# Position table by half-array products, no bias by TensorE in the steady batches, second norm a batch later, last batch written out

## The reference

```
qkv = LN(x) @ W_qkv + b_qkv                      # 16 heads of 8
scores = q k^T / sqrt(8) + rel_bias[clip(i - j + 128, 0, 256)]
attn = softmax(scores) v ; y = attn @ W_out + b_out
x = x + LN(y)
h = silu(LN(x) @ w1^T * s1) * (LN(x) @ w2^T * s2)      # 128 -> 512
h = gelu(h @ h1^T * h1s) ; h = gelu(h @ h2^T * h2s)    # 512 -> 512, ternary weights
x = x + LN(h @ w3^T * w3s)                       # 512 -> 128
```

## Time and profile before

| | before |
|---|---|
| median of 3 runs | 291.06 us (290.31 to 291.15) |
| the profiled execution | 290.61 us, its span in the trace 288.8 us |
| mean granted clock of TensorE | 0.992 |
| busy: PE, DVE, ACT, POOL | 267.7, 212.5, 205.2, 102.5 us |

### The profile page before, as it was taken

How to read it: one execution, slowest core, us unless ns; L and a number is a source line. 1 busy time by engine, 2 the same in 40 slices (tenths; PEclk the granted TensorE clock), 3 DMA queues, 4 the chain that set the end, 5 groups by cost and what they waited for, 6 DMA issues and landing times.

```text
span 288.8 us, 5174 instructions
## 1 busy us (share of the span) xinstructions
PE 267.7 (93%) x1875; PEld 180.7 (63%) x1875; DVE 212.5 (74%) x442; ACT 205.2 (71%) x316; POOL 102.5 (35%) x107
## 2 busy tenths in 40 slices
PE   7899989899999999999999998999999999999980
PEld 7656646555555555556555554557888888888860
DVE  4576977889789789789788888857654853673675
ACT  2677777785876776785886886767459976896750
POOL 6716000101702603923974985117640202400111
PEclk9999999999999999999999999999999999999996
DMA  6979505322221262560221200000000000010012
GB/s 159 339 231 142 184 5 183 129 65 90 64 84 41 74 194 103 179 210 21 75 78 36 78 0 3 1 3 1 0 2 0 0 0 2 0 36 2 2 36 77
DMA packets 21356, 21.17 MB, mean 73 GB/s; under 512 B 3664, under 2 KB 18768, under 8 KB 21072
## 3 DMA queue, kind: packets, MB, share of 16 engines
q1 hardware_dynamic: 20464, 20.53, 24.4%
q10 hardware_dynamic: 864, 0.27, 0.4%
HBM read 14.90 MB, written 5.64 MB: 71 GB/s over the span
## 4 chain that ended last, share of the span: by engine, by line
PE 68%; DVE 16%; ACT 8%; issue 5%; DMA 1%; POOL 1%; ACTq 0%; POOLq 0%; DVEq 0%
PE place L1449 11%; PE place L1450 11%; PE place L1252 10%; PE pv L1304 7%; DVE mx L692 6%; PE place L1244 5%; ACT ring L1016 4%; PE place L1278 4%; DVE place L699 3%; PE place L1203 2%; PE misc L1315 2%; PE place L1289 2%; PE misc L1182 2%; PE pv L1450 2%; PE pv L1449 2%
## 5 line engine op out<-in xcount | busy, mean ns | idle before, releaser
L692 DVE TENSOR_REDUCE mx<-place 128x4 f32<-128x1024 f32 x64 | 78.3, 1223 | 16.2 <-PE place L1252 14.9
L517 POOL TENSOR_TENSOR rstd<-mv,mhalf 128x2 f32<-128x2 f32 (+1 forms) x26 | 20.9, 806 | 145.8 <-DVE mv L624 145.8
L1016 ACT ACTIVATE ring<-place 128x1024 f32<-128x1024 f32 x64 | 65.7, 1028 | 6.4 <-PE place L1289 3.1
L1252 PE MATMUL place<-room,identr 128*128 128x512 f32 x128 | 47.0, 448 | 0.0
L1023 ACT COPY place<-raw 128x1024 f32<-128x1024 f32 x37 | 37.8, 1024 | 11.7 <-DVE mx L692 11.7
L1449 PE MATMUL place<-room,w_hi 128*128 128x512 f32 (+1 forms) x116 | 44.7, 387 | 0.7 <-DVE room L825 0.7
L1450 PE MATMUL place<-room,w_hi 128*128 128x512 f32 (+1 forms) x116 | 44.1, 383 | 0.0
L1304 PE MATMUL pv<-ring,vx 128*9 128x256 f32 x512 | 33.6, 380 | 0.4 <-ACT ring L1016 0.4
L825 DVE TENSOR_TENSOR room<-ring,room 128x512 fp32r<-128x512 f32 x32 | 21.3, 690 | 17.1 <-ACT room L1104 17.1
L1244 PE MATMUL place<-room 33*128 33x256 f32 x256 | 28.4, 298 | 4.9 <-ACT ring L1016 4.8
L1278 PE MATMUL place<-room 33*128 33x256 f32 x256 | 31.7, 328 | 1.4 <-DVE place L699 1.1
(11 more groups left out here) (141 smaller groups left out, 434.4 us busy)
## 6 DMA issues: line engine op xcount, KB each, us to landing
raw<-ext SPq DMA_DIRECT2D x8, 384.0 KB, 6.8
room<-q_parts SPq DMA_DIRECT2D x48, 64.0 KB
room<-k_parts SPq DMA_DIRECT2D x48, 64.0 KB
w_lo<-h SPq DMA_DIRECT2D x2, 1024.0 KB, 5.6
q_parts<-w_hi SPq DMA_DIRECT2D x4, 256.0 KB, 3.0
k_parts<-w_hi SPq DMA_DIRECT2D x2, 512.0 KB, 3.4
xs<-x SPq DMA_DIRECT2D x3, 256.0 KB, 6.1
w_lo<-w SPq DMA_DIRECT2D x3, 256.0 KB, 2.8
```

The source lines that it names most:

```text
L517: nc.gpsimd.tensor_tensor(rstd[:, at:at + width], mv[:, at:at + width, 1], mhalf[:, 0:width], ALU.pow).then_inc(rstd_set, 1)
L692: nc.vector.tensor_reduce(mx[:, s // RPAIRS, :, :, s % RPAIRS].rearrange("p i k -> p k i"), max_tile(b * PAIRS + s)[:, :, :].rearrange("p ...
L1016: nc.scalar.activation(probs[:, s % PRING, :, :, :].rearrange("p k j n -> p (k j n)"), score_tile(b * PAIRS + s)[:, :, :].rearrange("p k n ...
L1252: last = mm(max_tile(b * PAIRS + s)[:, half, :], identr[:, :], windows(table_hi[:, 2 * s + half, :], 0, P, 2, S), start=False, stop=True, ...
```

## The change

1. **Max bias in halves** (`bias_product`). The table holds, for head 0 of a pair, 64 partitions x 448 columns in partitions 0 to 63, and for head 1 the same in 64 to 127 (`load_halves`). The identity `ident_wide` is 64 rows x [zeros, identity, zeros]. Four products of 64 rows and 512 columns take the place of two of 128 rows.
2. **No bias by PE** in batches 0 to 6: for s = 7 ACT copies it too (a sixth copy in each batch). In the last batch PE does s = 6.
3. **Table loads.** The half tables (16 loads, into the free end of `w_lo`) come first; the full `raw` (8 loads) is loaded after `store_parts(1)` and ahead of `row_dmas(1)`.
4. **z a batch later.** Two places for z; `norm_T`, `keep_zT` and `z_low` run for batch b-2.
5. **The last batch** is written out on PE, DVE and ACT; DVE copies the bias of steps 1, 2, 3, 4, 5 and 7; `BLANKS` go from (2, 2, 2, 6, 6) to (0, 0, 0, 2, 6), and three blank streams stand elsewhere (4 products in b = 0, 4 in b = 5, 2 in b = 6).

```diff
-BY_PE = (7,)
+BY_PE = ()
 BY_DVE = (2, 5)
-LAST_BY_DVE = (1, 2, 4, 5, 6)
+LAST_BY_PE = (6,)
+LAST_BY_DVE = (1, 2, 3, 4, 5, 7)
...
-        BLANKS = (2, 2, 2, 6, 6)
+        BLANKS = (0, 0, 0, 2, 6)
...
+        def load_halves(eng, s):
+            for half in range(2):
+                eng.dma_start(raw_halves[half * HP:(half + 1) * HP, s, :],
+                              bass.AP(tensor=ext.tensor, offset=(2 * s + half) * EXT,
+                                      ap=[[1, HP], [1, TWIN]])).then_inc(table_in[s], 16)
...
             store_parts(1)
+            for s in range(PAIRS):
+                load_table(sp, s)
             sp.wait_ge(parts_out[1], PARTS_OUT)
             row_dmas(1, 0, PAIRS, second_rows_in)
...
+            def bias_product(tile, table, s, block, half):
+
+                at = half * HP
+                return mm(tile[:, half, :], ident_wide[at:at + HP, HP - block * HP:3 * HP - block * HP],
+                          windows(table[at:at + HP, s, :], block * HP, P, 2, S), start=False, stop=True,
+                          skip_group_check=True)
+
             def max_bias(b, s):
                 if b == 0:
                     pe.wait_ge(table_hi_pool, s + 1)
-                for half in range(2):
-                    last = mm(max_tile(b * PAIRS + s)[:, half, :], identr[:, :],
-                              windows(table_hi[:, 2 * s + half, :], 0, P, 2, S),
-                              start=False, stop=True, skip_group_check=True)
+                for block in range(2):
+                    for half in range(2):
+                        last = bias_product(max_tile(b * PAIRS + s), table_hi, s, block, half)
                 last.then_inc(ms_ready, 1)
...
             def second_norm(b):
                 dve.wait_ge(rstd_set, b * 2 + NU + 2)
-                if b > 0:
-                    dve.wait_ge(zT_ready, b)
+                if b > 1:
+                    dve.wait_ge(zT_ready, b - 1)
                 for t in range(TPB):
-                    last = normalize(z[:, t, :], xs[:, b * TPB + t, :], t)
+                    last = normalize(z[b][:, t, :], xs[:, b * TPB + t, :], t)
...
+            first = (B - 1) * PAIRS
+            write_bias(first + 2)
+            weigh(B - 2, 0)
+            write_bias(first + 3)
+            write_bias(first + 4)
+            write_bias(first + 5)
+            weigh(B - 2, 1)
+            largest_low()
+            write_bias(first + 7)
+            attn_moments(B - 2)
+            any_low()
+            residual(B - 2)
+            z_low(B - 3)
+            second_norm(B - 2)
...
+            last_scores(6)
+            weighted(B - 1, 2)
+            last_scores(7)
+            project(B - 2)
+            pe.wait_ge(y_read, B - 1)
+            pe.wait_ge(w_low_top_set, 2)
+            mm(misc[0:1, 0:P], w_low_top[:, :], ident[:, :], start=True, stop=True).then_inc(w_low_row, 1)
+            pe.wait_ge(w_low_any_set, 1)
+            norm_T(B - 3)
+            weighted(B - 1, 3)
```

More of the change, by code:

```diff
@@ L55 @@
 SLOT_HEAD = [s + HALF * k for s in range(PAIRS) for k in range(2)]
[L58 removed]
+BY_PE = ()
 BY_DVE = (2, 5)
[L60 to L61 removed]
+LAST_BY_PE = (6,)
+LAST_BY_DVE = (1, 2, 3, 4, 5, 7)
+LOW_PAIRS = BY_PE + tuple(s for s in LAST_BY_PE if s not in BY_PE)
 def windows(ap, start, step, count, width):
@@ L239, in build @@
         rows_set = sem("rows_set")
+        table_in = [sem(f"table_in{s}") for s in range(PAIRS)]
         table_hi_pool = sem("table_hi_pool")
@@ L1038, in _ @@
             write_bias(0)
-            for b in range(B):
+            for b in range(B - 1):
                 for s in range(PAIRS):
                     ahead = b * PAIRS + s + 1
-                    if ahead < B * PAIRS and ahead % PAIRS in by_act(ahead // PAIRS):
+                    if ahead % PAIRS in by_act(ahead // PAIRS):
                         write_bias(ahead)
@@ L1279, in scores @@
                                   rows(k_rows, b, half, s)[:, j * P:(j + 1) * P], rows(q_rows, b, half, s),
[L1280 to L1281 removed]
+                                  start=(s in by_pe(b) and j == 0), stop=False, skip_group_check=True)
+                if s not in by_pe(b):
                     last.then_inc(st_ready, 1)
             def score_bias(b, s):
[L1285 to L1290 removed]
+                low = LOW_PAIRS.index(s)
+                pe.wait_ge(table_lo_set, low + 1)
+                for table, at in ((table_hi, s), (table_lo, low)):
+                    for block in range(2):
+                        for half in range(2):
+                            last = bias_product(score_tile(b * PAIRS + s), table, at, block, half)
                 last.then_inc(st_ready, 1)
@@ L1360, in _ @@
             v(2)
-            for b in range(B):
-                more = b + 1 < B
+            for b in range(B - 1):
                 for s in range(PAIRS):
-                    if more or s not in BY_PE:
-                        scores(b, s)
-                    if s == 6 and 1 <= b <= 4:
+                    scores(b, s)
+                    if s == 6 and b > 0:
                         pe.wait_ge(mrow_set, b * RANGES + 3)
@@ L1376, in _ @@
                             v(4)
-                    if more:
-                        max_scores(b + 1, s)
-                        max_bias(b + 1, s)
-                    if s in BY_PE and more:
+                        if b == 5:
+                            stream(misc, blank, blank, 4)
+                        if b + 2 == B:
+                            norm_T(b - 2)
+                    max_scores(b + 1, s)
+                    max_bias(b + 1, s)
+                    if s in BY_PE:
                         score_bias(b, s)
-                    if s + 1 in BY_PE and not more:
-                        scores(b, s + 1)
-                        score_bias(b, s + 1)
                     if s == 0:
@@ L1426, in _ @@
                             v(3)
-                    if s == 5 and more:
+                    if s == 5:
                         if b == 0:
```

199 lines of the change are left out of this document (125 added, 74 removed).

## The result

Slower: 299.2 us in the median of four runs (295.6 to 302.9) against 291.0 for the kernel before beside it, a ratio of 1.025 (95% interval 1.021 to 1.028). The prediction was 284.3, with 280.5 to 289.5 as its range. Ratios here rest on the undisturbed runs of both kernels, so they can differ a little from the ratio of the medians. The profiled execution took 299.58 us, its span 297.8.

The account below looks back on a forecast made before the run. PE, two thirds of the chain, with DVE close behind it, was taken to bound the kernel. Start 0, batches -1.3 - 1.1 - 3 x 1.5 - 2 x 0.3, last batch +0.5 + 0.3 gave -6.7 us: 284.3, range 280.5 to 289.5.

Parts of the forecast that it names:

- 19.5 or 19.6: Predicted batch length in us, with DVE busy over 90%; step 7's exponentials 19.5 us apart in batches 1 to 6.
- The copy by ACT: Step 7: ACT's sixth copy is hidden and L1289's 0.94 us leaves the chain, starting the exponential 0.93 us sooner.
- third rival: Max bias: half products do not overlap, so the kernel gets slower, +8 us to 299; chance 0.06.
- z a batch later: 0: Step 7: the later z takes PE's transposes and DVE's z_low off fresh data, which stood in DVE's pause; 0 us.
- The start: 0 to 33 us: PE gains about 0 and some 6 us of slack cover the table loads; 0, bounds -0.5 and +3.
- First scores after 35: Start: a stated sign that the prediction is wrong; it expected first scores at 33.3 us.
- the early queue ends some 3.9 us sooner: Start, DMA: half tables are 1.8 MB where full ones are 3.1, at 340 GB/s.
- fourth rival: Start: loads back and the maxima's row land 5 to 8 us late behind the tables; 290 to 293 us, chance 0.08.
- The blank streams taken out lay in waits: Last batch: the removed blank streams stood in PE's waits; no time was counted for them.
- the steps on step 7 and on z: Batches: L1289's 0.94 us leaves the chain in batches 0 to 4; moving z's transposes a batch later counts 0.
- "+0.5" and "+0.3": Last batch: first FFN product 0.5 us later, then DVE's residual and second_norm +0.3; bounds -1 and +2.
- the estimate of 190.5: Last batch: project starts at about 190.5 us, from six copies, eight exponentials and job order; first FFN product at about 194.4.

Follow-up runs that it names:

- e6: e5 with the last batch in its order of before the change and z of batch 5 transposed in batch 6's step 7; 283.28 us, ratio 0.974.
- e7: The kernel before, max bias in full rows, with ACT's sixth copy and four zero products at step 7 in batches 0 to 6; 287.8 us, ratio 0.989.
- e3: The kernel before with only BY_PE = (): ACT copies the bias of step 7 in every batch, no half products; 294.9 us, ratio 1.017.
- e10: e6 with z transposed in the batch after it, as before the change; 283.26 us.
- e4: The changed kernel with the half tables of two pairs in one load, 8 issues for 16; 294.1 us, ratio 1.010.
- e1: The changed kernel with the eight full table loads issued behind the first maxima's row; 294.8 us, ratio 1.015.
- e2: The kernel before plus six 384 KB table loads, read by nobody, behind store_parts(1); 291.14 us, ratio 1.001.
- e5: e1b with e4's merged loads and batch 1's maxima row sent ahead of W_out's loads and unit 3's stores; 288.9 us, ratio 0.990.
- e1b: e1 with four zero products at step 7 of batches 0 to 6 and more blank streams in the rebuilt last batch; 291.55 us, ratio 1.001.
- e8: e6 without the added zero products (two in batch 6 stay); four runs of 283.7 to 295.8 us, ratio 0.984 without the longest.
- e9: e5 with six zero products ahead of each of the last batch's weighted sums; 289.6 us, ratio 0.995.

## Why the prediction was wrong

**What held: the length of the batches, in part by luck.** "19.5 or 19.6" was 19.40 in every undisturbed batch 2 to 4. In e6, with the clock up throughout, batches 0 to 6 gained 1.5, 1.2, 1.7, 1.7, 1.7, -0.1 and 0.4, together 8.1 us where the steps said 7.5. But the two terms behind this sum were both off. The copy by ACT, counted at some 0.93 us in each of batches 0 to 4 (4.7 in all), brought 0.4 to 1.0 in each, 2.8 in all (e7 and e3 alike). The rest of the change to the steady batches, for which that leaves 2.8 of the forecast's 7.5, brought 5.3 (e6 against e7). The errors cancel; no run shows why the halves bring more than their borders. That pairs of half products overlap did hold. PE's timeline after, in batch 3:

```profile
105.45 0.40 PE L1320 MATMUL place<-room 33*128 33x256 f32 x4
105.69 0.63 PE L1327 MATMUL place<-room 64*128 64x512 f32 x4
106.25 0.66 PE L1397 MATMUL misc<-ident,oT 128*128 128x128 f32 x4
...
107.18 0.40 PE L1320 MATMUL place<-room 33*128 33x256 f32 x4
107.42 0.63 PE L1327 MATMUL place<-room 64*128 64x512 f32 x4
107.98 0.40 PE L1386 MATMUL pv<-ring,vx 128*9 128x256 f32 x4
```

From L1320 to the weighted sum is 107.98 - 107.18 = 0.80 (0.81 predicted, 0.99 in the earlier trace rows), so pairs of half products overlap fully, and the third rival falls. Into a transpose it is 106.25 - 105.45 = 0.80 as well, not the 0.91 predicted: the extra 0.10 for a change of weights behind the max bias did not come, and the transposes gain 0.09 too. DVE is busy 91% of batch 3's window, as said (85% and 87% in e6's batches 2 and 6, though), and PE 18.2 us, not 17.5.

**z a batch later: 0.** e10 shows it, within 0.4 us. It does take the transposes out of step 7 of batch 1, one of the places where PE then stands still (below).

**The start: "0", with +3 as its bound; it was +6.4.** "First scores after 35", the prediction's own sign of being wrong, came: 39.43. The step counted bytes ("the early queue ends some 3.9 us sooner") and forgot that half tables are sixteen issues, not eight. SP needs 0.61 us for each, so its list, not the DMA engines, set the pace up to 18 us: the engines moved 162 GB/s from 8 to 18 us in after, at a busy share of 0.58, where the kernel before has 346 at 1.05. The rate taken over from the earlier trace rows was too high as well: e4, with its engines at 1.03 in the same stretch, moved 246. The loads back then went out 4.1 us later and behind 3.1 MB of full tables. Neither part alone makes all of it. With fewer issues (e4) or without the tables ahead (e1) 4.4 or 5.4 of the 6.4 us come back, and bytes alone on the old issue list (e2) cost nothing. The prediction's fourth rival had the symptom, a row that lands late behind the tables, but from a slow table rate; all DMA together ran at 307 GB/s from 20 to 27 us, not under 200.

**The clock: no step at all.** This is the largest miss. In batch 0 the wait for the row put TensorE on 1.2 GHz until 48.6: the batch took 21.18 where e6 has 17.93, +3.25 (e4, with this order and the clock up, took 18.36, so 2.8 of it are the clock's). In batch 2 it is +1.5, in batch 6 23.43 against e6's 19.54, +3.9. Together that is 8.6 us of the 16.7 by which after's FFN starts later than e6's (202.98 - 186.28), 8.2 of them the clock's; the start is 5.9, the last batch 2.15. What failed is that the sum prices work taken from PE as time alone. "The blank streams taken out lay in waits" says so for the last batch; the steady batches had no blank streams before, and there it is the steps on step 7 and on z that take L1289 and some transposes away without a term for PE then standing still. PE's timeline after, at the end of batches 1 and 5 and in the last batch:

```profile
81.07 0.50 PE L1360 MATMUL place<-room 33*128 33x256 f32 x4 [0.96 <-ACT place L1082]
...
160.90 0.50 PE L1360 MATMUL place<-room 33*128 33x256 f32 x4 [0.90 <-ACT place L1082]
...
190.45 0.51 PE L1360 MATMUL place<-room 33*128 33x256 f32 x4 [1.81 <-DVE place L738]
```

The clock fell at 82.8, 161.3 and 192.0, 0.4 to 1.7 us behind the ends of these stops. Before the change PE had L1289 and a transposed z at the first two of these places, and no stop there but one of 0.55 and 0.45 us a microsecond later, which after has too (0.45); after, the first place has neither and the second has only the transpose. In e6 added zeros stand at the first:

```profile
70.92 0.74 PE L1240 MATMUL pv<-blank 128*128 128x256 f32 x4
71.95 0.51 PE L1354 MATMUL place<-room 33*128 33x256 f32 x4 [0.30 <-ACT place L1076]
```

Over all the traces, between 30 us and the FFN, the clock fell 21 times, and 19 of these falls lie in a stop of PE of 0.81 us or more or at most 2.6 us behind one. The kernel before, e2, e7 and e10 have no such stop and no fall. The stop does not settle it alone: eleven such stops had no fall behind them (1.79 us in e4, 1.06 in e6), and two falls had no such stop in front (e5 at 72.4; e3 at 174.9, behind one of 0.53). e1b against e1 (3.2 us less with more products of zeros), e8 against e6 (4.2 us more by the medians with fewer) and e3 show that less work on PE costs clock; that it does so through these stops is read from the traces, and no run has changed one stop alone. The Trainium skill's TensorE: Matmul & The Clock Gate (A second HAM failure mode) describes a kernel in which short idle gaps between groups of matmuls let the clock go up and down. The trace agrees that it can happen without a long wait, with the falls behind the stops of 0.96 and 0.90 us; no run here shows which stop or which product decides.

**The last batch: "+0.5" and "+0.3".** To the FFN it was +2.1 in after and +4.9 in e5; `project` came 14.9 us after batch 6's last exponential, where the estimate of 190.5 meant 13.4 after 177.13. The tail behind it was sized right, 4.0 us for 3.9, so what was mis-sized is the way to `project`. In it stands a wait that the estimate did not have, PE's 1.81 us for DVE's bias copy, and in each of the five other runs with this order the clock fell within 1.5 us of its end as well. In after up to 1.7 us can be the clock, which was low for 3.4. e9 against e6 is cleaner: 5.1 us more, of which its 12 more zero products are at most 1.9 (six take 0.97) and its low stretch at most 1.7. At least 1.5 us are left for the order. How much of them is the wait for DVE's copy was not tried.

**The sum.** e6 took 283.35 in its profiled execution where 283.9 was forecast, but it is another kernel, with the start, the last batch and the clock put right, and two wrong terms that cancel lie under the forecast: the agreement is luck in part. As made, the change spent e6's gain twice over: 5.9 + 2.15 + 8.6 = 16.7 us against 7.6.

## What to carry to other kernels

When large loads are split, count issues as well as bytes: price each DMA of a queue that others stand behind at its issue time, and look at what lies behind the last of them. Products taken out of TensorE's waits were not free here: look at the granted clock beside every batch's length, and if it has holes, look for the stop of PE ahead of each and try zero products there. When a forecast is met, check its terms too and not the sum alone. Change the order of steady batches and that of the last batch in separate versions, since the one can hide the other's gain.

## What the runs showed of the hardware

- TensorE's granted clock fell from 1.00 to 0.50 in stretches of 3.4 to 24 us, 19 of 21 times in or shortly behind a stop of PE of 0.81 us or more, in steady batches too, and stayed low while PE was busy (9.8 of 10.2 us from 161.3 in after). The runs of one kernel differ in it: four runs of after had mean clocks of 0.951, 0.945, 0.937 and 0.930, and took 295.6, 298.8, 299.6 and 302.9 us. Such kernels scattered more, by 2.5% (after), 2.1% (e4) and 4.3% (e8), where the kernel before, e6 and e7, with no hole before the end, stay within 0.5%; e10, without one too, by 0.9%; but e1, with four holes in its profiled execution, kept within 0.7%, so a small scatter does not rule them out.
- Two products of 64 rows and 512 columns on different halves of the array's rows run side by side: four take 0.56 us from start to start of what follows, as long as two of 128 rows ahead of a transpose (0.56), and eight take 1.03 (e6, from 181.37 to 182.40), so the second four add 0.47.
- SP issued a load of 64 partitions x 448 columns in 0.61 us (2.45 / 4), one of 128 partitions x 2 x 384 in 0.59 (4.69 / 8), so the smaller load is not cheaper to issue.
